# Where a head's q and k are projected, and where the reciprocals stand among the maxima: a two-block transformer kernel on one core

## The reference, cut to what matters

```python
q, k, v = heads(xn @ Wq), heads(xn @ Wk), heads(xn @ Wv)      # 16 heads of 64
att = einsum('bhid,bhjd->bhij', q, k) / 8 + alibi_bias        # 1024 x 1024 each
p   = softmax(att, axis=-1)
out = einsum('bhij,bhjd->bhid', p, v)                         # then out @ Wo
```

## Time and profile before

| | us |
|---|---|
| median of 3 runs (lowest, highest) | 3428.2 (3427.2, 3432.61) |
| the profiled execution's own time | 3427.71 |
| its span, first to last instruction | 3425.9 |
| PE busy in the span | 2955.4 (86%) |
| DVE busy | 2152.8 (63%) |
| POOL busy | 1737.6 (51%) |
| ACT busy | 1523.4 (44%) |

### The profile page before, as it was taken

How to read it: one execution, slowest core, us unless ns; L and a number is a source line. 1 busy time by engine, 2 the same in 40 slices (tenths; PEclk the granted TensorE clock), 3 DMA queues, 4 the chain that set the end, 5 groups by cost and what they waited for, 6 DMA issues and landing times.

```text
span 3425.9 us, 43451 instructions
## 1 busy us (share of the span) xinstructions
PE 2955.4 (86%) x13360; PEld 1893.8 (55%) x13360; DVE 2152.8 (63%) x3692; ACT 1523.4 (44%) x1974; POOL 1737.6 (51%) x954
## 2 busy tenths in 40 slices
PE   4799999788779999978877999997887799999787
PEld 3555555566545555556655555555665455555565
DVE  5556666477555666647745666665774556666577
ACT  1245555255225555535522555553552355554354
POOL 2045555477205555547710555564770155556476
PEclk7899999899879999989977999998997899999799
DMA  3000000010100000000010000000101000000100
GB/s 134 2 7 7 9 7 7 17 37 28 46 2 9 7 9 7 6 27 28 28 46 3 8 8 8 9 3 27 37 18 46 3 8 9 7 9 4 36 28 24
DMA packets 23389, 65.54 MB, mean 19 GB/s; under 512 B 3796, under 2 KB 13012, under 8 KB 23128
## 3 DMA queue, kind: packets, MB, share of 16 engines
q1 hardware_dynamic: 23288, 64.24, 5.7%
HBM read 62.10 MB, written 4.22 MB: 19 GB/s over the span
## 4 chain that ended last, share of the span: by engine, by line
PE 68%; DVE 13%; issue 9%; ACT 6%; POOL 2%; DMA 0%; DVEq 0%; ACTq 0%; SPq 0%; POOLq 0%
PE P L1276 13%; PE P L1239 9%; PE P L1264 6%; PE P L1261 6%; PE P L1361 4%; PE P L1220 4%; PE P L1362 3%; PE P L1363 3%; PE P L1226 3%; DVE Kb L789 2%; PE P L1340 2%; DVE mhalf L793 2%; PE P L1163 2%; ACT Ka L921 2%; PE P L1284 2%
## 5 line engine op out<-in xcount | busy, mean ns | idle before, releaser
L793 DVE TENSOR_REDUCE mhalf<-P 128x1 f32<-128x512 f32 x1024 | 664.4, 686 | 316.6 <-PE P L1226 183.5
L949 ACT ACTIVATE pfull<-P 128x1024 f32<-128x1024 f32 x512 | 523.7, 1023 | 635.9 <-PE P L1264 632.3
L447 POOL TENSOR_TENSOR opair<-opair,pfull 128x1024 f32<-128x1024 f32 x192 | 455.6, 2373 | 164.1 <-ACT pfull L949 163.5
L447 POOL TENSOR_TENSOR spair<-spair,pfull 128x1024 f32<-128x1024 f32 x192 | 458.5, 2388 | 145.9 <-ACT pfull L949 141.8
L1276 PE MATMUL P<-pfull,V 128*64 128x512 f32 x2048 | 495.0, 605 | 0.0
L1239 PE MATMUL P<-Ka,Qa 96*128 96x512 f32 x1024 | 417.9, 462 | 83.3 <-DVE Kb L789 39.7
L1361 PE MATMUL P<-Kb,R 128*128 128x512 f32 x864 | 379.9, 440 | 126.8 <-DVE Qb L834 125.3
L1261 PE MATMUL P<-Qa,Ka 98*128 98x512 f32 x1024 | 451.6, 441 | 5.4 <-ACT Qa L938 4.4
L1264 PE MATMUL P<-Qb,Kb 128*128 128x512 f32 x1024 | 433.7, 424 | 0.0
L834 DVE TENSOR_TENSOR Qb<-A,Kb 128x512 fp32r<-128x512 f32 x288 | 302.0, 1048 | 172.0 <-ACT Kb L1025 172.0
L1239 PEld LDWEIGHTS P<-Ka,Qa 96*128 96x128 f32 x1024 | 192.4, 192 | 324.4 <-DVE mhalf L793 243.9
(11 more groups left out here) (205 smaller groups left out, 4334.5 us busy)
## 6 DMA issues: line engine op xcount, KB each, us to landing
wex<-in_wex SPq DMA_DIRECT2D x40, 768.0 KB, 4.2
Ka<-auxrows SPq DMA_DIRECT2D x64, 128.0 KB, 2.2
wpair<-in_whead SPq DMA_DIRECT2D x64, 96.0 KB, 2.0
modb<-modrows SPq DMA_DIRECT2D x4, 768.0 KB, 6.3
A<-in_x SPq DMA_DIRECT2D x5, 512.0 KB, 3.4
x<-in_x SPq DMA_DIRECT2D x4, 512.0 KB, 3.3
out_x<-x SPq DMA_DIRECT2D x4, 512.0 KB, 2.7
A<-in_consts SPq DMA_DIRECT2D x1, 1872.0 KB, 15.5
```

The costliest lines, as they stand in the source:

```text
L447: pool.tensor_tensor(psum8[s][:, :], psum8[s][:, :], pfull[:, j % RING, :], ALU.add).then_inc(S["p_added"], 1)
L793: dve.tensor_reduce(mhalf[:, i, t:t + 1], P[:, 6 + i, :], AX.X, ALU.max, negate=True).then_inc(S["max_red"], 1)
L949: act.activation(pfull[:, j % RING, :], banks(2 * (j % 2)), ACT.Exp, scale=DH1 ** -0.5).then_inc(S["exp_done"], 1)
```

## The change

It does two things. First, q and k of head n+2 (not n+1) are projected at the end of head n, behind its last weighing and ahead of the next head's scores(0). So in step 0 of head n+1 no projection stands any more, and ACT's copies of q and k stand, both, in step 7 behind the copy of the maxima's rows and ahead of the next head's first exponential. A `project_qk` for head 1 is added ahead of the first pair. Second, the maxima's tiles stand in steps 1 to 6 (before: 2 to 6), and DVE's four reciprocals stand behind the reductions of tiles 3, 4, 5 and 6 (before: behind `m_mid`). The number of instructions with work in them is the same on every engine.

```diff
-MAX_TILES = [([], []), ([], []), ([], [0]), ([1], [2]), ([3], [4]), ([5], [6]), ([7], []), ([], [])]
+MAX_TILES = [([], []), ([], [0]), ([], [1]), ([2], [3]), ([], [4]), ([5], [6]), ([7], []), ([], [])]
+INVERT_AT = 3
...
# DVE, prep(s, n, done, pair)
                             dve.tensor_reduce(mhalf[:, i, t:t + 1], P[:, 6 + i, :], AX.X, ALU.max, negate=True).then_inc(S["max_red"], 1)
+                        if done is not None and INVERT_AT <= t < INVERT_AT + NINV:
+                            invert(s, done, t - INVERT_AT)
...
                     if done is not None:
-                        for c in range(NINV):
-                            invert(s, done, c)
                         normed(s, done, pair)
...
# ACT, pair
-                        if ahead and jj == 0:
-                            q_high(1 - s, n + 1)
                         if ahead and jj == T - 1:
                             maxima(1 - s, n + 1)
+                            if not is_last:
+                                q_high(s, n + 2)
+                                k_high(s, n + 2)
                             if s == 1:
                                 values(p + 1, 0)
...
-                        if ahead and jj == 0:
-                            k_high(1 - s, n + 1)
...
# PE, pair
-                        if ahead and jj == 0:
-                            project_qk(1 - s, n + 1)
...
                             weigh(k, T - 1, s, n, p)
+                            if not is_last:
+                                project_qk(s, n + 2)
...
# PE, ahead of the first pair (ACT likewise: q_high(1, 1), k_high(1, 1) ahead of its first exponential)
                 turn_max(0)
+                project_qk(1, 1)
                 scores(0, 0, 0, 0)
```

More of the change, by code:

```diff
@@ L995, in _ @@
                 maxima(0, 0)
+                q_high(1, 1)
+                k_high(1, 1)
                 exps(0, 0, 0)
```

## The result

The changed kernel takes 3455.93 us (median of 6 runs, 3453.01 to 3456.36) against 3428.34 for the kernel before (6 runs): a ratio of 1.0077, 95% interval 1.0064 to 1.0090. It is slower by 27.6 us. The forecast was 3443, 15 us slower, with a range to 3455; the median lies 0.9 us above that range. The sign and the two places of the loss inside the loops were right. About half of the loss sits in a third place, which the forecast booked as a small gain.

What follows compares the result with a forecast made beforehand. PE was taken to set the pace. 28 pairs at +0.58 us (+16.2) and four heads 0 (-1.4) gave +14.9 us on the profiled 3427.71, so 3443 us as median; eight-in-ten range 3419 to 3455.

Steps and rivals of the forecast that it cites:

- What bounds the kernel, and which waits the change touches: PE sets the pace, busy 54.51 of 57.00 us; touched are tile 0's waits for k and the waits for reductions.
- The start of scores(2): It waits for ACT's first exponential, 1.02 us in B and 0.62 in A, starting at T + 5.17 and T + 5.66.
- T: The zero of a head's timetable: end of the previous head's last weighing, where the moved projection starts.
- The first halves: From T to X: the new wait ahead of scores(2) replaces waits ahead of scores(3) and tile 0; B -0.34, A +0.06 us.
- B: A head that follows one with s = 0; its first half was forecast to win 0.34 us.
- A: A head that follows one with s = 1, with both halves of V projected in it; first half forecast to lose 0.06 us.
- X: The start of tile 5 of the maxima on PE, from which the second half of a head is counted.
- The lag behind the third reciprocal: On DVE between the reductions of tiles 5 and 6: it delays tile 7 and everything behind, +0.43 us a head.
- `mneg` and `m_mid` between POOL's adds: DVE's small steps on the maxima start between two POOL adds, so no wait for the shared port; `mneg` takes 0.17 us.
- Rival 4: DVE's last step on the maxima falls behind POOL's add; 56 heads lose 2.05 us each, 3558 us; chance 0.05.
- The pair: One A and one B head together: -0.34 + 0.06 + 2 x 0.43 = +0.58 us, so 57.4 us.
- Four heads 0 at -0.34 each: Head 0 of each batch has B's first half but no reciprocals; -1.4 us for the four.

Runs made afterwards that it cites:

- `e4_old_tile_places`: The changed kernel with the maxima's tiles back in their old steps (2 to 6): 3443.9 us, ratio 1.0045.
- `e1_recips_last`: The changed kernel with the four reciprocals back behind the last step on the maxima: 3437.2 us, ratio 1.0027.
- `e2_recips_only`: The kernel before with only the reciprocals moved behind tiles 3 to 6, projection and tiles as before: 3442.6 us, ratio 1.0041.
- `e8_tiles_even`: `e5_table_recips_last` with the maxima's tiles in steps 1 to 5, none left in step 7: 3565.1 us, ratio 1.0399.
- `e5_table_recips_last`: The changed kernel with the reciprocals back at the end and a tiny early exponential that loads the table: 3416.0 us, ratio 0.9964.
- `e3_table_early`: The changed kernel with a one-element exponential ahead of ACT's work for head 0, loading the table there: 3428.8 us, ratio 1.0001.
- `e6_fill_wait`: The changed kernel with 8 matmuls of zeros ahead of scores(2) in head 0 of each batch, table load unmoved: 3443.5 us, ratio 1.0044.

## Why the prediction was right or wrong

1. **What bounds the kernel, and which waits the change touches**: right. The wait for k is gone, and scores(2) waits instead.
2. **The start of scores(2)**: right, T + 5.19 and T + 5.68 for 5.17 and 5.66.
3. **The first halves**, B -0.34 and A +0.06: mis-sized. Measured at X in the two heads shown they are 18.06 - 18.32 = -0.26 and 19.49 - 19.29 = +0.20, over all 28 heads of each kind -0.23 and +0.18. The projection alone comes nearer to the forecast: in `e4_old_tile_places`, against the kernel before, X is 0.28 sooner in B and 0.11 later in A. The rest is a term that the prediction put at nothing, "Spreading the tiles over steps 1 to 6 wins nothing in return": it costs 0.05 to 0.07 a head, 3.6 us in the loops. What in the new order costs it was not traced. The two waits of before were read partly from modelled ends, which may hold the remaining 0.05 a head.
4. **The lag behind the third reciprocal**, +0.43: mis-sized, and outside its bounds of 0.38 to 0.48. scores(7) moved from X + 4.02 to X + 4.27 or 4.28, so 0.26 a head. The prediction set the reductions, the reciprocal and the reductions end to end. In the trace the reciprocal starts 0.09 before the reductions end and tile 6's reductions start 0.08 before it ends, and they take 1.22 where 1.30 was counted. The kernel before has this overlap already, between neighbours of one kind: its four reciprocals take 3.38 us, and each is 0.89 to 0.94 long. `e1_recips_last` and `e2_recips_only` show 0.25 to 0.26 a head in either kernel, and tile 7's wait grew to 0.76, not 0.9.
5. **`mneg` and `m_mid` between POOL's adds**: right, 0.17 in 60 of 64 heads, and turn_max waits in none of the loops' heads. Rival 4 did not happen here. `e8_tiles_even`, which brought those steps forward to fall behind an add, took 149 us more than `e5_table_recips_last`, the clock's part included.
6. **The pair**: 29.32 + 27.95 = 57.27, forecast 57.4, before 56.81. The misses of steps 3 and 4 have opposite signs (+0.23 and -0.35 a pair), so the sum in the loops, +13.0 for +16.2, is better than its terms. That is luck.
7. **Four heads 0 at -0.34 each**: this step failed. They were taken to have head B's first half. Measured are +2.65, +4.17, +4.29 and +2.44, 13.6 us together, a little more than in all loops. Two things were overlooked. In head 0 ACT changes to the exponential's table, which stood ahead of its copies and now stands behind them, on the path (1.28 us). And behind the longer wait the granted clock falls to 0.50, which costs 3.9 us more on average. `e3_table_early` and `e6_fill_wait` show both. Without the two, heads 0 win 1.8 us each (`e3_table_early` against the kernel before), not 0.34; why was not settled. With this term at its measured size, the sum would have been 16.2 + 13.6 = +29.8. With every term as measured it is 14.3 - 4.9 + 3.6 + 13.6 + 1.9 = +28.5.
8. **Other stages at zero**: +1.9 us in the profiled execution, of which no cause was shown.

## What to carry to other kernels

Follow a moved instruction not only in the loop but in the iteration that enters it: there an engine may still owe a one-time cost (here a table load of 1.3 us) that had cover at the old place. A wait of PE can cost more than its length through the clock: here the waits of 1.59 to 2.24 us in heads 0 did, and so did half of the waits of 2.5 us in the loops of `e8_tiles_even`, while those of 1.12 us and less did not. Filling such a wait with matmuls kept the clock. And before small DVE steps with two SBUF inputs are moved, look where POOL's large adds fall; a reduction, or an operand in PSUM, took them out of that contest here. Last, let one experiment differ by one part of a change only: three parts with opposite signs (+14.3, -4.9, +3.6) looked like one here.

## What the runs showed of the hardware that was not expected

- The granted clock fell from 1.00 to 0.50 (1.2 GHz) behind a wait of 2.24 us in head 0, though PE was busy again after it, and came back at about 202 us, 9 us after the wait's end. With matmuls on zeros in the same gap (seven in the trace) it stayed at 1.00.
- Waits of nearly one length (1.59 to 1.61 us, the four heads 0 of `e1_recips_last`) were followed by low-clock stretches of 3.4 or about 10 us, so the same wait cost different times.
- Neighbours on DVE overlap in the traces by 0.08 to 0.09 us, of one kind (two reductions, two reciprocals) or of two (reduction and reciprocal, both ways), so a chain of them is shorter than the sum of their lengths.
- A table load of 1.28 us was followed by its exponential within 0.01 us.
- Two DVE steps on 8 columns took 2.09 and 2.19 us instead of 0.17, each until an add of POOL's ended; in the version with a reduction and PSUM the same steps took 0.17 to 0.18 inside an add.
